# A selective scan beside a mixture of experts: TensorE spreads delta first in each slot, and du three units ahead of the scan

## The chip, the cores and the metric

The kernel runs on one NeuronCore of a Trainium2 chip. Its time is the device time of one execution in microseconds (us), as a median over runs. All times of the trace come from one profiled execution. The engines are named as the profile names them: PE is TensorE, DVE is VectorE, ACT is ScalarE, POOL is GpSimd, SP is the queue that issues most DMAs.

## What is computed

The input holds 32 sequences of 256 tokens of 128 numbers. After a layer norm, two blocks are added to it: a Mamba-like block with a selective scan, and a mixture of 8 experts. The scan is what matters here:

```python
def step(s, inp):
    d_t, u_t, B_t, C_t = inp
    dA = jnp.exp(d_t[..., None] * A)
    s = s * dA + (d_t * u_t)[..., None] * B_t[:, :, None, :]
    y_t = jnp.einsum('bhdn,bhn->bhd', s, C_t)
    return (s, y_t)
...
y = y + x * Dskip
y = y * jax.nn.silu(z)
out = y @ out_proj_w.T
```

There are 256 inner channels d and 16 states n for each, so 4096 recurrences run over the tokens. `delta` (`d_t` above) is a softplus of a projection of x; du stands for `d_t * u_t`. The experts are two matrix products with a relu between them, on 1024 gathered rows each.

## The kernel before

**Chunks, units, slots.** The tokens are cut into 16 chunks (`CHUNKS`) of 512. In a chunk the 4096 recurrences are 32 units (`SLOTS`) of 128 partitions: 8 channels times 16 states. Unit w of a chunk takes four steps, each one instruction on a tile of 128x512:

- PE spreads du, 8 channels to 128 partitions, with a 0/1 matrix `sel_d` (`spread_du`, L1243), into one of two PSUM banks (`du_ps[w % 2]`). It spreads delta in the same way (`spread_delta`, L1250), into one of three banks (`decay_of(w)`).
- ACT makes the decay, exp(delta * A), in place in that bank (L863).
- DVE multiplies the spread du by B (`spread_u`, L1020), which makes `u_sb`, and runs the scan over decay and `u_sb` (L1075).
- POOL multiplies the result by C (L647), and four units at a time are summed by PE (`sum_quad`, L1265).

**Order within an engine.** Every engine has a written-out order, a loop over chunks and 32 slots a chunk, and waits on semaphores. In its slot w, DVE first does `spread_u` of unit w+1, then the scan of unit w, then what else is due (the gates, L1000 and L1004, in slots 4 and 5 of each half of a chunk, and the addition of the output projection, L1011). ACT makes the decay of unit w in its slot w and then all other activations that are due. PE in its slot w first spreads for unit w+2 (`AHEAD = 2`), du and then delta, then sums a quad where one is due, and then does the parts of other tiles that the tables of the planner put into this slot.

**What the spreads wait for.** A du spread for unit v needs its bank read by DVE: it waits until `u_sb` of unit v-2 is made (`u_ready`). A delta spread for unit v needs its bank read by the scan of unit v-3 (`scan_done`). Since the three decay banks start anew in each chunk, the delta spread of a chunk's unit 0 waits for unit 30 of the chunk before, that of unit 1 for unit 31, and that of unit 2 finds its bank long free.

```python
wait(pe, "u_ready", per_chunk(ch, SLOTS, w - 1))
...
last = w - 2 if w >= 3 else (-1, 0, -2)[w]
wait(pe, "scan_done", per_chunk(ch, SLOTS, last))
```

**The other tiles.** In parallel with the scan of a chunk, PE makes the tiles of the next chunk, in two PSUM banks (`misc`): z0 and x0 (L1161, L1158; x takes four matmuls, `in_proj`), from them bc0 and v0 (L1169, `x_proj`), the softplus part D0 (L1178, L1180, `delta`), and the same for half 1 (z1, x1, bc1, v1, D1). Their slots are in `STAGE_A`: z0 in slot 4 and read by ACT in its slot 6, v0 in slot 9, z1 in 13, x1 in slots 11 to 14 and read in slot 16, v1 in 23. ACT's silu of z and x (`silus`, L726, L728, L730) loads its function table and puts the old one back, 1.28 us each. After v come the steps of the softplus (`softplus_step`, L748 to L762). In chunks 2 to 14 the experts' tiles (L1207 to L1218 on PE, L779 to L801 on ACT) are in slots of their own (`FFN_AT`); this table repeats after three chunks. `outp` (L1192) is the output projection, in slots 18 and 19. The first halves' D tiles of chunks 0 to 2 are taken further by DVE (`scale_x`, L1027), later ones by POOL (L587).

In what follows "unit 7" is unit 7 of its chunk, and slots are PE's slots if not said otherwise.

Of the kernel before, what the change touches and what calls it, by code (L numbers as in the profile page):

```python
# [34 lines left out]
CHUNKS = TOK // CH  # L35
# [5 lines left out]
SLOTS = HALVES * UNITS  # L41
# [5 lines left out]

HELP = {0: 1, 1: 1, CHUNKS - 1: 1}
SUM = QUADS + 2
AHEAD = 2  # L50
EXP, FF = 8, 512
CAP = TOK // EXP
FT = FF // P
# [72 lines left out]
def bass_mamba_moe(nc, hidden, in_w, conv_w, conv_b, xp_w, dt_w, dt_b, a_log, d_skip, out_w,  # L126
                   wg, w1, b1, w2, b2, consts, out):
    ctx = ExitStack()
    with ctx:
# [209 lines left out]
        def per_chunk(ch, n, k):  # L339
            return ch * n + k  # L340
# [12 lines left out]
        def wait(eng, name, value):  # L353
            if not isinstance(value, int) or value > 0:
                eng.wait_ge(S[name] if isinstance(name, str) else name, value)
# [11 lines left out]
        def head_of(w):  # L367

            return w % QUADS // 2

        def group_of(w):

            return w % 2 * QUADS + w % UNITS // QUADS
# [36 lines left out]
        def decay_of(w):  # L410
            return decay[w % len(decay)]
# [692 lines left out]
        def _(pe):  # L1104
# [117 lines left out]
            def tile_part(x, part):  # L1222

                if part == 0:
                    claim(x)
                if x.kind in ("x", "z"):
                    in_proj(x, part)
                elif x.kind == "D":
                    delta(x, part)
                elif x.kind in ("bc", "v"):  # L1230
                    x_proj(x)
                elif x.kind == "outp":
                    out_proj(x, part)
                else:
                    expert(x, part)

            def spread_du(ch, w):

                hf = w // UNITS
                if w % UNITS == 0:  # L1240
                    pe.wait_ge(S["stacked"], per_chunk(ch, 128, 64 * (hf + 1)))
                wait(pe, "u_ready", per_chunk(ch, SLOTS, w - 1))
                pe.matmul(du_ps[w % 2][:, :], sel_d[:, group_of(w), :, :].rearrange("k n d -> k (n d)"),  # L1243
                          dsp[:, hf, head_of(w), 1, :], start=True, stop=True).then_inc(S["du_spread"], 1)

            def spread_delta(ch, w):

                last = w - 2 if w >= 3 else (-1, 0, -2)[w]
                wait(pe, "scan_done", per_chunk(ch, SLOTS, last))
                pe.matmul(decay_of(w)[:, :], sel_d[:, group_of(w), :, :].rearrange("k n d -> k (n d)"),  # L1250
                          dsp[:, w // UNITS, head_of(w), 0, :], start=True, stop=True
                          ).then_inc(S["delta_spread"], 1)

            def spread(ch, w):
                spread_du(ch, w)
                spread_delta(ch, w)

            def sum_quad(ch, k):

                r = k % (UNITS // QUADS)  # L1260
                if r == 0:
                    wait(pe, "g_ready", per_chunk(ch, 2, k * QUADS // UNITS))
                wait_products(pe, ch, QUADS * (k + 1))
                for q in range(QUADS):
                    mm = pe.matmul(y_ps[q * 32:(q + 1) * 32, :], con[:, K_SUM + 32 * r:K_SUM + 32 * (r + 1)],  # L1265
                                   s_sb[:, (QUADS * k + q) % S_RING, :],
                                   start=(r == 0), stop=(r == UNITS // QUADS - 1))
                mm.then_inc(S["sum_done"], 1)
# [78 lines left out]
            first_tile("bc", 1)  # L1347
            first_tile("v", 1)
            pe.wait_ge(S["route_dve"], 5)
            for w in range(AHEAD):  # L1350
                spread(0, w)

            for ch in range(CHUNKS):
                for w in range(SLOTS):
                    if w + AHEAD < SLOTS:
                        spread(ch, w + AHEAD)
                    elif ch + 1 < CHUNKS:
                        spread(ch + 1, w + AHEAD - SLOTS)
                    if (w - SUM) % QUADS == 0:
                        if w >= SUM:  # L1360
                            sum_quad(ch, (w - SUM) // QUADS)
                        elif ch > 0:
                            sum_quad(ch - 1, (w - SUM) // QUADS + SLOTS // QUADS)
                    for x, part in parts_at.get(ch * SLOTS + w, []):
                        tile_part(x, part)
# [49 lines left out]
```

## Time and profile before

| | |
|---|---|
| median of 3 runs | 1085.64 us (1085.16 to 1087.5) |
| the profiled execution | 1085.05 us |
| its span, first to last instruction | 1083.2 us |
| mean granted TensorE clock | 0.956 |
| busy: DVE | 1014.2 us, 94% of the span |
| busy: PE matmuls / weight loads | 962.7 us, 89% / 440.5 us, 41% |
| busy: POOL | 898.0 us, 83% |
| busy: ACT | 747.5 us, 69% |
| one scan (L1075), one product for u_sb (L1020), 512 each | 1213 ns, 671 ns in the mean |
| the mean DMA rate | 99 GB/s |

The busy shares are averages over the whole program. The main loop over the units runs from 59.5 us, when DVE first makes `u_sb`, to 1068 us, when it has begun the last scan. Matmuls are pipelined, so the share of PE is not that of its peak; a matmul's start and end in the trace overlap those of its neighbours. An instruction's idle time is that of its engine just before it, with the engine or transfer whose signal ended it.

### The profile page before, as it was taken

What the parts mean: (1) busy time and instruction counts of PE and PEld (TensorE: products, weight loads), DVE (VectorE), ACT (ScalarE), POOL (GpSimd) and SP (SyncE); (2) the same over time, 40 slices, a digit from 0 to 9 for tenths busy, and PEclk for the clock granted to TensorE, in tenths of its full rate; (3) what the DMA queues carried; (4) which work ended last, traced back from release to release, by engine and by line L of the source; (5) the groups of instructions that cost most, each with busy time, mean ns of one, the idle gap of its engine ahead of it and who ended that gap; (6) DMA issues with size and microseconds to landing.
All of it is one profiled execution on the core that took longest, in us unless ns stands there. A gap on an engine that the chain in (4) does not pass through costs nothing.

```text
span 1083.2 us, 11968 instructions
## 1 busy us (share of the span) xinstructions
PE 962.7 (89%) x3521; PEld 440.5 (41%) x3521; DVE 1014.2 (94%) x1371; ACT 747.5 (69%) x1198; POOL 898.0 (83%) x783
## 2 busy tenths in 40 slices
PE   6978778799899999989999999999999999998785
PEld 3433223344444444434344444434444444443232
DVE  7789999999999999999999999999999999999995
ACT  5666465577887777786776877786787778786331
POOL 5458888997989898888888988888898888889874
PEclk8988998989999999999999999999999999999866
DMA  9584244344335342432533352243354233237821
GB/s 271 163 214 93 71 102 105 74 113 94 82 78 126 79 88 49 115 66 68 122 83 83 68 123 63 56 114 83 78 119 94 46 83 75 57 79 165 193 64 49
DMA packets 77452, 106.99 MB, mean 99 GB/s; under 512 B 8734, under 2 KB 46540, under 8 KB 77388
## 3 DMA queue, kind: packets, MB, share of 16 engines
q1 hardware_dynamic: 72944, 97.74, 40.5%
q0 software_dynamic: 4096, 8.46, 2.3%
q8 instruction: 29, 0.48, 0.2%
q14 instruction: 35, 0.29, 0.1%
q10 hardware_dynamic: 348, 0.03, 0.0%
HBM read 17.99 MB, written 21.10 MB: 36 GB/s over the span
## 4 chain that ended last, share of the span: by engine, by line
PE 35%; DVE 26%; issue 17%; ACT 15%; POOL 7%; DMA 0%; POOLq 0%; DVEq 0%; ACTq 0%
DVE u_sb L1020 11%; DVE s_sb L1075 8%; PE bank L1213 5%; PE bank L1250 4%; PE bank L1158 4%; PE bank L1265 4%; POOL s_sb L647 4%; PE bank L1243 4%; PE bank L1178 4%; ACT bank L863 3%; PE bank L1210 3%; PE bank L1169 2%; ACT L730 2%; ACT L726 2%; POOL moe L620 1%
## 5 line engine op out<-in xcount | busy, mean ns | idle before, releaser
L647 POOL TENSOR_TENSOR s_sb<-s_sb,c_of 128x512 f32<-128x512 f32 x488 | 625.0, 1290 | 122.2 <-DVE s_sb L1075 116.5
L1075 DVE TENSOR_TENSOR_SCAN s_sb<-bank,u_sb 128x512 f32<-128x512 f32 x512 | 620.9, 1213 | 14.2 <-ACT bank L863 14.0
L863 ACT ACTIVATE bank<-bank,a_neg 128x510 f32<-128x510 f32 x512 | 332.3, 663 | 213.4 <-PE bank L1250 211.7
L1020 DVE TENSOR_TENSOR u_sb<-bank,b_of 128x512 f32<-128x512 f32 x512 | 343.5, 671 | 24.9 <-PE bank L1243 23.8
L1243 PE MATMUL bank<-dsp,sel_d 128*128 128x512 f32 x512 | 326.3, 637 | 18.1 <-DVE u_sb L1020 16.7
L1250 PE MATMUL bank<-dsp,sel_d 128*128 128x512 f32 x512 | 228.2, 446 | 55.0 <-DVE s_sb L1075 51.9
L1243 PEld LDWEIGHTS bank<-dsp,sel_d 128*128 128x128 f32 x512 | 100.1, 195 | 194.3 <-DVE u_sb L1020 103.0
L1250 PEld LDWEIGHTS bank<-dsp,sel_d 128*128 128x128 f32 x512 | 100.2, 196 | 182.0 <-DVE s_sb L1075 136.6
L1265 PE MATMUL bank<-s_sb,con 128*32 128x512 f32 x1024 | 144.9, 639 | 17.4 <-POOL s_sb L647 13.4
L1158 PE MATMUL bank<-xnT,wx 128*128 128x512 f32 x256 | 133.8, 608 | 0.0
L653 POOL DMA_INDIRECT expert_in<-xn,put_at x64 | 70.1, 1096 | 11.6 <-issue 11.3
L620 POOL DMA_INDIRECT moe<-xn x64 | 64.7, 1010 | 12.9 <-issue 9.2
L1210 PE MATMUL bank<-xn 128*128 128x512 f32 x128 | 66.4, 611 | 4.7 <-ACT xn L779 4.7
L597 POOL TENSOR_TENSOR dd<-dd,hi 128x1024 fp32r<-128x1024 f32 x27 | 64.0, 2369 | 7.1 <-ACT hi L775 7.1
L1213 PE MATMUL bank<-xn 128*128 128x512 f32 x128 | 63.3, 602 | 0.0
L1158 PEld LDWEIGHTS bank<-xnT,wx 128*128 128x128 f32 x256 | 47.8, 192 | 27.1 <-issue 19.4
L785 ACT ACTIVATE xn<-bank,b1c 128x512 f32<-128x512 f32 x64 | 43.6, 700 | 18.8 <-PE bank L1210 18.8
L726 ACT ACT_TABLE_LOAD x32 | 41.1, 1283 | 15.4 <-PE bank L1161 15.0
L1265 PEld LDWEIGHTS bank<-s_sb,con 128*32 128x32 f32 x1024 | 20.9, 110 | 59.4 <-issue 39.1
L1192 PEld LDWEIGHTS bank<-wzo,g_sb 128*128 128x128 f32 x256 | 35.1, 204 | 18.0 <-issue 15.9
L730 ACT ACT_TABLE_LOAD x32 | 41.1, 1283 | 0.6
L1178 PE MATMUL bank<-sp_e,con 128*128 128x512 f32 x64 | 34.8, 626 | 6.7 <-ACT xn L785 6.0
(143 smaller groups left out, 1014.2 us busy)
## 6 DMA issues: line engine op xcount, KB each, us to landing
b_of<-bc SPq DMA_DIRECT2D x64, 256.0 KB, 5.5
c_of<-bc SPq DMA_DIRECT2D x64, 256.0 KB, 5.9
dsp<-hi SPq DMA_DIRECT2D x64, 256.0 KB, 4.1
dsp<-dd SPq DMA_DIRECT2D x64, 256.0 KB, 4.7
expert_in<-fill SPq DMA_DIRECT2D x16, 260.0 KB, 5.4
xn<-expert_in SPq DMA_DIRECT2D x8, 520.0 KB, 5.3
moe<-fill SPq DMA_DIRECT2D x8, 512.0 KB, 6.8
xn<-L_ffn_W SPq DMA_DIRECT2D x16, 256.0 KB, 5.0
```

Source lines behind the costliest of these rows:

```text
L620: pool.indirect_dma_start(moe[:, :], bass.IndirectOffsetOnAxis(ap=xe[:, e % 2, th * CT + q, DM + 1:ROWX].bitcast(U32), axis=0), eo[:, th, ...
L647: pool.tensor_tensor(s_now, s_now, c_of[:, hf, hh, :], ALU.mult).then_inc(S["p_ready"], 1)
L863: act.activation(d, d, ACT.Exp, scale=a_neg[:, k:k + 1]).then_inc(S["decay_ready"], 1)
L1020: dve.tensor_tensor(u_sb[:, w % U_RING, :], du_ps[w % 2][:, :], b_of[:, hf, head_of(w), :], ALU.mult).then_inc(S["u_ready"], 1)
L1075: dve.tensor_tensor_scan(s_sb[:, w % S_RING, :], decay_of(w)[:, :], u_sb[:, w % U_RING, :], 0.0, ALU.mult, ALU.add).then_inc(S["scan_done" ...
L1158: mm = pe.matmul(t[:, :], wx[:, hf, part, :], xnT[:, seqs, part:part + SEQ], start=(part == 0), stop=(part == TAPS - 1))
L1178: pe.matmul(t[:, :], ident, (sp_e, sp_r, sp_a)[part], start=(part == 0), stop=False)
L1210: mm = pe.matmul(t[:, :], w1_sb[:, b, x.k * P:(x.k + 1) * P], xeT, start=True, stop=True)
L1213: mm = pe.matmul(t[:, :], w2_sb[:, b, part, :], hT[:, part, :], start=(part == 0), stop=(part == FT - 1))
L1243: pe.matmul(du_ps[w % 2][:, :], sel_d[:, group_of(w), :, :].rearrange("k n d -> k (n d)"), dsp[:, hf, head_of(w), 1, :], start=True, stop= ...
L1250: pe.matmul(decay_of(w)[:, :], sel_d[:, group_of(w), :, :].rearrange("k n d -> k (n d)"), dsp[:, w // UNITS, head_of(w), 0, :], start=True ...
L1265: mm = pe.matmul(y_ps[q * 32:(q + 1) * 32, :], con[:, K_SUM + 32 * r:K_SUM + 32 * (r + 1)], s_sb[:, (QUADS * k + q) % S_RING, :], start=(r ...
```

## The change

The function `spread` that put du before delta is gone, and so is `AHEAD`. In its slot w, PE now spreads delta for unit w+2 first, as far ahead as before, and then du for unit w+3. Ahead of the loop du is spread for one more unit. The banks and what each spread waits for stay as they are: a du spread still waits for `u_sb` of the unit two before it, which for unit w+3 is unit w+1.

```diff
-AHEAD = 2
+
+DELTA_AHEAD, DU_AHEAD = 2, 3
...
-            def spread(ch, w):
-                spread_du(ch, w)
-                spread_delta(ch, w)
...
-            for w in range(AHEAD):
-                spread(0, w)
+            for w in range(DELTA_AHEAD):
+                spread_du(0, w)
+                spread_delta(0, w)
+            for w in range(DELTA_AHEAD, DU_AHEAD):
+                spread_du(0, w)
...
                 for w in range(SLOTS):
-                    if w + AHEAD < SLOTS:
-                        spread(ch, w + AHEAD)
-                    elif ch + 1 < CHUNKS:
-                        spread(ch + 1, w + AHEAD - SLOTS)
+                    for spread, ahead in ((spread_delta, DELTA_AHEAD), (spread_du, DU_AHEAD)):
+                        if w + ahead < SLOTS:
+                            spread(ch, w + ahead)
+                        elif ch + 1 < CHUNKS:
+                            spread(ch + 1, w + ahead - SLOTS)
                     if (w - SUM) % QUADS == 0:
```

The matmuls are the same; only their order on PE differs. Behind the spreads, PE's lines are numbered differently after the change (the du spread is L1244, the delta spread L1251, the sum of a quad L1262, and L1169 is L1170, L1213 is L1214, L1178 is L1179).

The first place is PE in slots 6 to 8 of chunk 5, around the scan of unit 7. Banks 3 and 4 hold du, 0 to 2 the decays, 5 the sums, 6 and 7 the other tiles. Before:

```order
L1243 MATMUL bank3<-dsp,sel_d 128x512 [waits u_ready]
L1250 MATMUL bank2<-dsp,sel_d 128x512 [waits scan_done]
L1265 MATMUL bank5<-s_sb,con 32x512 [waits p_ready,p_dve,g_ready]
L1265 MATMUL bank5<-s_sb,con 32x512 x3
L1243 MATMUL bank4<-dsp,sel_d 128x512 [waits u_ready]
L1250 MATMUL bank0<-dsp,sel_d 128x512 [waits scan_done]
L1169 MATMUL bank7<-xs,bcw 64x512 [waits misc_act]
L1213 MATMUL bank6<-xn 128x512 [waits misc_act]
L1243 MATMUL bank3<-dsp,sel_d 128x512 [waits u_ready]
L1250 MATMUL bank1<-dsp,sel_d 128x512 [waits scan_done]
L1213 MATMUL bank6<-xn 128x512 [waits misc_act] x2
```

And after the change:

```order
L1251 MATMUL bank2<-dsp,sel_d 128x512 [waits scan_done]
L1244 MATMUL bank4<-dsp,sel_d 128x512 [waits u_ready]
L1262 MATMUL bank5<-s_sb,con 32x512 [waits p_ready,p_dve,g_ready]
L1262 MATMUL bank5<-s_sb,con 32x512 x3
L1251 MATMUL bank0<-dsp,sel_d 128x512 [waits scan_done]
L1244 MATMUL bank3<-dsp,sel_d 128x512 [waits u_ready]
L1170 MATMUL bank7<-xs,bcw 64x512 [waits misc_act]
L1214 MATMUL bank6<-xn 128x512 [waits misc_act]
L1251 MATMUL bank1<-dsp,sel_d 128x512 [waits scan_done]
L1244 MATMUL bank4<-dsp,sel_d 128x512 [waits u_ready]
L1214 MATMUL bank6<-xn 128x512 [waits misc_act] x2
```

The spread that stands last ahead of a slot's other work, and so holds it back while it waits, was the delta spread with its wait for a scan; it is now the du spread with its wait for a product `u_sb`.

The second place is PE at the boundary between chunks 4 and 5 (slots 30 and 31 of chunk 4). Before:

```order
L1243 MATMUL bank3<-dsp,sel_d 128x512 [waits u_ready,stacked]
L1250 MATMUL bank0<-dsp,sel_d 128x512 [waits scan_done]
L1265 MATMUL bank5<-s_sb,con 32x512 [waits p_ready,p_dve]
L1265 MATMUL bank5<-s_sb,con 32x512 x3
L1210 MATMUL bank7<-xn 128x512 [waits misc_act]
L1243 MATMUL bank4<-dsp,sel_d 128x512 [waits u_ready]
L1250 MATMUL bank1<-dsp,sel_d 128x512 [waits scan_done]
```

And after the change:

```order
L1251 MATMUL bank0<-dsp,sel_d 128x512 [waits scan_done]
L1244 MATMUL bank4<-dsp,sel_d 128x512 [waits u_ready]
L1262 MATMUL bank5<-s_sb,con 32x512 [waits p_ready,p_dve]
L1262 MATMUL bank5<-s_sb,con 32x512 x3
L1211 MATMUL bank7<-xn 128x512 [waits misc_act]
L1251 MATMUL bank1<-dsp,sel_d 128x512 [waits scan_done]
L1244 MATMUL bank3<-dsp,sel_d 128x512 [waits u_ready]
```

The du spread of unit 1 (bank 4) has moved from behind the sum and an expert's matmul to ahead of them.

## Rows read from the trace of the kernel before

**Rows 1.** Stretches of the run: busy time of each engine, granted clock, DMA share, GB/s.
```profile
132.00:192.00 60.00, 49.16 (x164) 19.85 (x163) 59.57 (x72) 37.10 (x56) 52.76 (x45) 0.91 0.44 96
312.00:372.00 60.00, 56.53 (x215) 26.28 (x215) 57.86 (x70) 45.54 (x72) 51.36 (x43) 1.00 0.42 93
```

**Rows 2.** Who waited for whom, whole span: total us, times, longest.
```profile
DVE u_sb L1020 <- PE bank L1243: 23.8, 45, 1.9
DVE s_sb L1075 <- ACT bank L863: 14.0, 28, 1.0
```

**Rows 3.** Timeline, chunk boundary: start, us, engine, line, [idle before <-releaser].
```profile
387.00 0.49 PE L1250 MATMUL bank<-dsp,sel_d 128*128 128x512 f32 x1 [0.25 <-DVE s_sb L1075]
...
389.81 0.69 DVE L1020 TENSOR_TENSOR u_sb<-bank,b_of 128x512 f32<-128x512 f32 x1 [1.13 <-PE bank L1243]
```

**Rows 4.** Timeline, from tile z0 to the scan of unit 7 of chunk 5.
```profile
399.81 0.39 PE L1250 MATMUL bank<-dsp,sel_d 128*128 128x512 f32 x1
...
399.83 1.28 ACT L726 ACT_TABLE_LOAD   x1 [1.10 <-PE bank L1161]
...
400.04 0.40 PE L1243 MATMUL bank<-dsp,sel_d 128*128 128x512 f32 x1
...
403.61 1.23 ACT L863 ACTIVATE bank<-bank,a_neg 128x510 f32<-128x510 f32 x2
...
404.30 1.22 DVE L1075 TENSOR_TENSOR_SCAN s_sb<-bank,u_sb 128x512 f32<-128x512 f32 x1 [0.56 <-ACT bank L863]
```

**Rows 5.** Timeline, TensorE meets the scan, before and after unit 7.
```profile
401.95 1.21 DVE L1075 TENSOR_TENSOR_SCAN s_sb<-bank,u_sb 128x512 f32<-128x512 f32 x1
...
403.08 0.67 DVE L1020 TENSOR_TENSOR u_sb<-bank,b_of 128x512 f32<-128x512 f32 x1
...
403.22 0.50 PE L1250 MATMUL bank<-dsp,sel_d 128*128 128x512 f32 x1 [0.24 <-DVE s_sb L1075]
...
403.65 1.07 PE L1169 MATMUL bank<-xs,bcw 128*64 128x512 f32 x2
...
405.44 0.67 DVE L1020 TENSOR_TENSOR u_sb<-bank,b_of 128x512 f32<-128x512 f32 x1
...
406.08 1.88 PE L1213 MATMUL bank<-xn 128*128 128x512 f32 x4
...
410.18 0.69 ACT L748 ACTIVATE sp_a<-bank,b1c 128x512 f32<-128x512 f32 x1 [0.17 <-PE bank L1169]
```

**Rows 6.** Timeline, the scan of unit 17.
```profile
422.60 1.81 ACT L863 ACTIVATE bank<-bank,a_neg 128x510 f32<-128x510 f32 x3
423.29 1.22 DVE L1075 TENSOR_TENSOR_SCAN s_sb<-bank,u_sb 128x512 f32<-128x512 f32 x1 [0.95 <-ACT bank L863]
```

**Rows 7.** Who waited for whom, VectorE, 378 to 563 us.
```profile
DVE u_sb L1020 <- PE bank L1243: 5.2, 10, 1.1
DVE s_sb L1075 <- ACT bank L863: 3.4, 7, 1.0
```

**Rows 8.** Timeline, chunk 5, unit 28, and the boundary after it.
```profile
443.02 0.68 ACT L863 ACTIVATE bank<-bank,a_neg 128x510 f32<-128x510 f32 x1
...
443.99 1.21 DVE L1075 TENSOR_TENSOR_SCAN s_sb<-bank,u_sb 128x512 f32<-128x512 f32 x1
...
449.32 0.69 DVE L1020 TENSOR_TENSOR u_sb<-bank,b_of 128x512 f32<-128x512 f32 x1 [0.44 <-PE bank L1243]
```

**Rows 9.** Timeline, chunk 2: softplus part and unit 17; chunk 7: unit 28.
```profile
204.05 1.81 DVE L1027 TENSOR_TENSOR dd<-dd,xs 128x512 f32<-128x512 f32 x1 [0.55 <-ACT dd L769]
...
238.77 1.22 DVE L1075 TENSOR_TENSOR_SCAN s_sb<-bank,u_sb 128x512 f32<-128x512 f32 x1 [0.47 <-ACT bank L863]
...
565.43 0.71 ACT L863 ACTIVATE bank<-bank,a_neg 128x510 f32<-128x510 f32 x1
...
566.23 1.22 DVE L1075 TENSOR_TENSOR_SCAN s_sb<-bank,u_sb 128x512 f32<-128x512 f32 x1
...
567.96 0.69 DVE L1020 TENSOR_TENSOR u_sb<-bank,b_of 128x512 f32<-128x512 f32 x1 [0.51 <-PE bank L1243]
```

## The prediction

> **What bounds the kernel.** I read the stretches first, then the waits, then the timeline around every stall of VectorE (DVE). In a middle stretch of 60 us DVE is busy for 57.86 us and TensorE (PE) for 56.53 us; in an early one DVE is busy for 59.57 us [rows 1]. So DVE sets the pace, and what can be won in the middle is the little that it stands: 23.8 us in 45 waits for a du spread, 14.0 us in 28 waits for a decay from ScalarE (ACT) [rows 2]. The change aims at the first kind.
>
> The timeline shows where they arise. At a chunk boundary PE meets the scan (its delta spread starts at 387.00 us, just when the scan that it waits for has ended), then does a sum and an expert's matmul, and only then the next du spread; DVE gets it 1.13 us late [rows 3]. From there PE does not stand again until it has made tile z0. ACT stands 1.10 us for that tile, loads its tables and does two silus, and makes the decay of unit 7 only at 403.61 us; DVE waits another 0.56 us for it [rows 4]. That is the reading on which all else rests: **the second stall hangs from PE's work and ACT's, not from DVE's progress.** If the first stall goes, DVE arrives earlier at unit 7 and waits there longer, by the same 1.13 us. The same again ten units later: PE meets a scan, makes v0, ACT stands 0.17 us for it [rows 5] and is then busy without a gap to the decays at 422.60 us, where DVE waits 0.95 us, a du stall having come shortly before [rows 6].
>
> **What the change does to a meeting.** Where PE lags behind by more than about 0.6 us, the order matters little: both spreads are free to go. Where it has caught up, it now waits twice. Delta starts 0.06 us after the scan that it waits for (that ends at 401.95 + 1.21 = 403.16 us, delta starts at 403.22). The du spread behind it waits for the product that DVE makes right after that scan: it starts at 403.08 and ends at 403.75 us [rows 5]. With the same 0.06 us, du starts at 403.81, **0.59 us after delta**, and all other work of the slot stands behind it on PE; no other engine's queue is held, but ACT waits for these tiles. So a meeting costs up to 0.59 us on the path PE, ACT, decay, scan. At the meeting after unit 7 it is less, since PE comes a little late: the product ends at 405.44 + 0.67 = 406.11 us, du starts at 406.17, and, 0.43 us later (403.22 to 403.65 was the same step), the experts' matmul at 406.60 in place of 406.08 [rows 5]: 0.52 us.
>
> Two smaller prices. At a chunk boundary the delta spread of unit 0 waits for the youngest scan, while du of unit 1 needs a product that is long made; there the extra spread costs only its own time, 0.23 us (the distance of two spreads, 399.81 to 400.04) [rows 4]. And where the decay hangs directly from a delta spread, delta being first in its slot gives back that 0.23 us: 0.59 - 0.23 = 0.36 us. From below, a meeting costs nothing where the tile is not awaited; it could gain only the 0.23 us. From above it is 0.59 us, plus the gate operation where one stands ahead of the product on DVE. I take each place at what its own rows give.
>
> **The sum over one period.** The experts' plan repeats after three chunks; I follow 378 to 563 us, where DVE waits 5.2 us for du and 3.4 us for decays [rows 7]. For each stall I ask what comes late next:
> - boundary to unit 7 (stalls 1.13 + 0.56 us): they merge into one at unit 7, as z0 comes 0.23 us later: +0.23 us;
> - unit 7 to unit 17 (one du stall, and decay stalls up to the 0.95 us): they merge at unit 17, v0 comes 0.52 us later than the scan does: +0.52;
> - unit 17 to the boundary: here ACT's decay for unit 28 is made at 443.02 + 0.68 = 443.70 us and its scan starts at 443.99, so 0.29 us of the 0.59 us is hidden: +0.30. The du stall after it, 0.44 us at 449.32 [rows 8], goes for good: together -0.14;
> - boundary to unit 7 of chunk 6: +0.23;
> - unit 7 to 17 of chunk 6: three du stalls and one decay stall merge; PE is held there by a product of GpSimd (POOL) in place of a scan, so there is no meeting: 0;
> - to unit 7 of chunk 7: meeting with delta's 0.23 us back: +0.36;
> - to unit 17 of chunk 7, the same kind of meeting: +0.36;
> - to the end of chunk 7: the decay for unit 28 ends at 565.43 + 0.71 = 566.14 us, its scan starts at 566.23 [rows 9]: 0.09 us hidden, +0.50; the du stall of 0.51 us at 567.96 goes: together -0.01.
>
> Sum +1.55 us a period. The pattern runs from 238 to 977 us, four periods: +6.2 us. In chunks 0 to 2, DVE's own part of the softplus waits for ACT (0.55 us at 204.05), hanging from PE's work behind a boundary: three times 0.23, +0.7. The silus before unit 17 end just in time or late (0.47 us at 238.77) [rows 9]: three times 0.36, +1.1. In chunk 15 the longest du stall, 1.9 us [rows 2], goes, but the addition of the output projection, which DVE does two instructions later, waits for the matmuls that stood before that du spread; I take 0.
>
> Total 6.2 + 0.7 + 1.1 + 0 = +8.0 us on the profiled execution's 1085.05 us, so **1093.0 us**. That execution is 0.6 us under the median shown, well inside what the forecast can tell.
>
> **A rule weighed.** Rows 1 have PE busy for 56.53 of 60 us, and for 26.28 us with weight loads. The Trainium skill (page "Perfetto Trace Analysis", section "Identifying the Most-Contended Engine") says that matmul busy time is a poor measure and that TensorE's headroom is better judged by weight-load time. By it PE would have more than half its time free, DVE alone would bind, and its waits would be the thing to remove: the first rival, not my forecast. What speaks against it here is ACT standing for z0 and v0.
>
> **The rivals.**
> - *The du stalls go for good* (faster). Deciding point: whether, after a du stall is gone, the next decay is made early enough to keep DVE from standing there. If units 7 and 17 get their tiles early enough, 23.8 us less the 1.9 us of chunk 15: 1063 us; if half comes back, 1074 us. For it: in several units after a stall the decay has more than a microsecond in hand. Against it: the merged stalls above. 0.12.
> - *Handed back, nothing more.* The du stalls turn into decay stalls, and the second wait of a meeting is hidden, because PE soon lags again: 1085 us, within 2 us. 0.09.
> - *The clock falls.* The granted clock is 1.00 in the dense stretch and 0.91 where PE stands more [rows 1]. If PE's added waits took it to 0.91, its 56.5 us of 60 would become 62, 2 us over each 60, some 12 times: about 1085 + 25 = 1110 us. PE's waits grow by under 1% of the span, so 0.03.
> - *My forecast*, meetings on the path: 0.76. That the change doesn't do what it says has a part in it: the third unit of lead exists only where PE lags; after a meeting du is as early as DVE's product allows.
>
> **Numbers.** Low end: the second rival, 1085. High end: six meetings a period at the full 0.59 us and two boundaries at 0.23 us, +4.0 us, four times, with the start 1103; I take 1099, since two places show what they hide. Left out: the first rival (0.12), clock and extremes (0.06). A measurement of this kernel tells about 0.2% (2.2 us) from no change. Faster 0.12, same 0.09, slower 0.79.
>
> **What would show it.** DVE's waits for du (line 1020) fall from 23.8 to under 3 us. Its waits for decays (line 1075) rise from 14.0 to about 14 + 21 + 8 = 43 us, most at units 7 and 17. PE has new waits for `u_sb` at its du spread, about 0.3 us each in slots where it has caught up, in chunks 0, 1 and 15 too. DVE's busy time stays at 1014 us and the clock at 0.95. The forecast is wrong if the decay waits stay below 30 us, or if the meeting after unit 7 of chunk 5 doesn't show du about 0.6 us behind delta.

## The result, and the profile after

The changed kernel takes 1095.55 us (median of 5 runs, 1093.77 to 1099.08) against 1085.64 us (the same median with five runs of before). The ratio over the runs of both is 1.0088, with a 95% interval of 1.0065 to 1.0111. The forecast was slower, 1093.0 us, between 1085 and 1099. The profiled execution of after took 1098.07 us (span 1096.2 us, mean granted clock 0.953), 2.5 us more than its median. So the trace shows a loss of 13.0 us where the runs show 9.9; both are used below, and not mixed.

The page's busy times, after:

```profile
PE 969.6 (88%) x3521; PEld 442.3 (40%) x3521; DVE 1011.2 (92%) x1371; ACT 745.3 (68%) x1198; POOL 897.7 (82%) x783
```

Stretches of after (us, busy PE, PEld, DVE, ACT, POOL, granted clock, DMA share, GB/s), for [rows 1]:

```profile
132.00:192.00 60.00, 45.78 (x161) 19.70 (x163) 58.61 (x71) 35.72 (x54) 52.85 (x44) 0.97 0.44 97
312.00:372.00 60.00, 56.60 (x212) 25.69 (x213) 56.83 (x68) 45.01 (x72) 50.66 (x42) 1.00 0.42 92
```

DVE's busy time is 1.03 us lower in the second stretch and PE's the same: nothing works longer, DVE stands longer. The waits of the whole span of after (us in total, times, longest), for [rows 2]:

```profile
PE bank L1244 <- DVE u_sb L1021: 52.1, 58, 3.4
DVE s_sb L1076 <- ACT bank L864: 43.6, 39, 1.9
PE bank L1251 <- DVE s_sb L1076: 30.0, 60, 1.2
DVE acc L1012 <- PE bank L1196: 8.2, 2, 5.6
...
DVE s_sb L1076 <- issue: 4.0, 8, 0.5
...
DVE u_sb L1021 <- PE bank L1244: 0.5, 2, 0.3
```

The waits for du went from 23.8 to 0.5 us, and those for decays from 14.0 to 43.6 us. So 23.3 us were taken away and 29.6 us came back on the other wait; 38.3 us of it, in 33 waits, stand between 250 and 980 us. The 4.0 us that the profile puts down to nothing ("issue") are decay waits too: all eight are at unit 28, and each of these scans starts 0.09 us after ACT has made its decay. The addition of the output projection (L1012) waits 2.8 us longer than before. PE's waits for products are not all new either, since before had these:

```profile
PE bank L1243 <- DVE u_sb L1020: 16.7, 14, 3.4
```

The long decay waits stand at two kinds of place. This is the first in after, from z0 to unit 7 of chunk 5 and the meeting behind it (for [rows 4, 5]):

```profile
404.64 1.28 ACT L727 ACT_TABLE_LOAD   x1 [1.34 <-PE bank L1162]
...
405.60 0.50 PE L1244 MATMUL bank<-dsp,sel_d 128*128 128x512 f32 x1 [0.34 <-DVE u_sb L1021]
...
408.42 1.81 ACT L864 ACTIVATE bank<-bank,a_neg 128x510 f32<-128x510 f32 x3
...
409.11 1.22 DVE L1076 TENSOR_TENSOR_SCAN s_sb<-bank,u_sb 128x512 f32<-128x512 f32 x1 [1.85 <-ACT bank L864]
...
410.39 0.50 PE L1251 MATMUL bank<-dsp,sel_d 128*128 128x512 f32 x1 [0.52 <-DVE s_sb L1076]
...
410.97 0.50 PE L1244 MATMUL bank<-dsp,sel_d 128*128 128x512 f32 x1
411.31 1.88 PE L1214 MATMUL bank<-xn 128*128 128x512 f32 x4
...
415.41 0.69 ACT L749 ACTIVATE sp_a<-bank,b1c 128x512 f32<-128x512 f32 x1 [0.17 <-PE bank L1170]
```

ACT stands 1.34 us for z0 (1.10 before) and makes the decay of unit 7 3.78 us after the table load begins, exactly as long as before. The stalls of 1.13 and 0.56 us have merged into one of 1.85 us. At the meeting du comes 0.58 us behind delta. ACT gets v0 6.30 us after unit 7's scan began, before 5.88 us (410.18 - 404.30): 0.42 us later. The second place, for [rows 6]:

```profile
427.83 1.81 ACT L864 ACTIVATE bank<-bank,a_neg 128x510 f32<-128x510 f32 x3
428.52 1.22 DVE L1076 TENSOR_TENSOR_SCAN s_sb<-bank,u_sb 128x512 f32<-128x512 f32 x1 [1.51 <-ACT bank L864]
```

1.51 us in place of 0.45 and 0.95 us.

### The profile page after: what moved, and what is told of

Same layout as the page of the kernel before. It is cut to its first block, busy times and chain, and to the rows that moved or that the text cites. A ratio compares the mean times of both kernels' runs of the same rounds, so it can differ in the third digit from the quotient of the medians.

```text
span 1096.2 us, 11968 instructions
## 1 busy us (share of the span) xinstructions
PE 969.6 (88%) x3521; PEld 442.3 (40%) x3521; DVE 1011.2 (92%) x1371; ACT 745.3 (68%) x1198; POOL 897.7 (82%) x783
## 4 chain that ended last, share of the span: by engine, by line
PE 38%; ACT 23%; DVE 19%; issue 16%; POOL 3%; DMA 0%; POOLq 0%; DVEq 0%; ACTq 0%
DVE u_sb L1021 10%; ACT bank L864 6%; PE bank L1159 5%; PE bank L1244 5%; PE bank L1262 4%; PE bank L1251 4%; PE bank L1214 4%; PE bank L1179 3%; PE bank L1170 3%; PE bank L1211 3%; ACT L731 3%; ACT L727 3%; DVE s_sb L1076 2%; POOL s_sb L648 2%; PE bank L1162 2%
## 5 line engine op out<-in xcount | busy, mean ns | idle before, releaser
L1076 DVE TENSOR_TENSOR_SCAN s_sb<-bank,u_sb 128x512 f32<-128x512 f32 x512 | 619.7, 1211 | 49.4 <-ACT bank L864 43.6
L1251 PE MATMUL bank<-dsp,sel_d 128*128 128x512 f32 x512 | 320.9, 627 | 30.3 <-DVE s_sb L1076 30.0
L1244 PE MATMUL bank<-dsp,sel_d 128*128 128x512 f32 x512 | 226.8, 443 | 59.3 <-DVE u_sb L1021 52.1
L1251 PEld LDWEIGHTS bank<-dsp,sel_d 128*128 128x128 f32 x512 | 100.6, 196 | 231.8 <-DVE s_sb L1076 142.0
L1244 PEld LDWEIGHTS bank<-dsp,sel_d 128*128 128x128 f32 x512 | 101.0, 197 | 166.5 <-DVE u_sb L1021 109.6
L1262 PE MATMUL bank<-s_sb,con 128*32 128x512 f32 x1024 | 144.8, 639 | 9.0 <-POOL s_sb L648 9.0
L786 ACT ACTIVATE xn<-bank,b1c 128x512 f32<-128x512 f32 x64 | 43.6, 700 | 30.3 <-PE bank L1211 30.3
L1214 PE MATMUL bank<-xn 128*128 128x512 f32 x128 | 63.4, 602 | 0.0
L1193 PEld LDWEIGHTS bank<-wzo,g_sb 128*128 128x128 f32 x256 | 35.2, 205 | 18.1 <-issue 16.7
L588 POOL TENSOR_TENSOR dd<-dd,xs 128x512 f32<-128x512 f32 x27 | 34.5, 1278 | 9.7 <-ACT dd L770 9.4
L1262 PEld LDWEIGHTS bank<-s_sb,con 128*32 128x32 f32 x1024 | 20.7, 109 | 50.6 <-issue 50.6
```

The source lines that it names most:

```text
L1076: dve.tensor_tensor_scan(s_sb[:, w % S_RING, :], decay_of(w)[:, :], u_sb[:, w % U_RING, :], 0.0, ALU.mult, ALU.add).then_inc(S["scan_done" ...
L1214: mm = pe.matmul(t[:, :], w2_sb[:, b, part, :], hT[:, part, :], start=(part == 0), stop=(part == FT - 1))
```

## How late the scan is, unit by unit

A loss that builds up slowly is best read from the start of the same scan in two traces. Each number is the start of one unit's scan in the timeline less its start before (before: 79.58, 209.93, 238.77, 404.30, 588.87, 958.00, 1020.22, 1049.22 us). The runs' names are explained below. "Net" is the last column less the first.

| | ch.0 unit 7 | ch.2 unit 3 | ch.2 unit 17 | ch.5 unit 7 | ch.8 unit 7 | ch.14 unit 7 | ch.15 unit 7 | ch.15 unit 21 | net |
|---|---|---|---|---|---|---|---|---|---|
| after | 0.34 | 0.33 | 2.56 | 4.81 | 6.47 | 10.69 | 12.04 | 12.72 | +12.4 |
| e1 | -0.06 | 0.16 | 2.06 | 3.86 | 5.82 | 9.65 | 9.85 | 10.30 | +10.4 |
| e11 | -0.06 | -0.02 | 1.73 | 2.30 | 2.23 | 2.12 | 2.88 | 1.14 | +1.2 |
| e2 | -0.13 | 0.18 | 0.86 | 0.92 | 0.79 | 0.59 | 1.22 | -0.15 | 0.0 |
| e4 | 0.45 | 0.49 | 0.98 | 0.89 | 0.83 | 0.63 | 0.99 | -0.41 | -0.9 |
| e6 | -0.61 | 1.32 | 0.44 | 3.56 | 6.93 | 13.80 | 16.27 | 14.66 | +15.3 |
| e9 | 1.56 | 1.63 | 0.36 | 0.00 | -0.04 | -0.09 | 0.49 | 0.53 | -1.0 |
| e7 | -0.89 | -0.84 | -0.66 | -1.99 | -2.69 | -4.01 | -3.22 | -5.18 | -4.3 |
| e5 | 1.48 | 2.27 | 2.22 | 1.23 | 0.16 | -1.98 | -1.83 | -2.47 | -4.0 |
| e10 | -0.32 | -0.08 | 0.65 | -1.67 | -3.42 | -6.95 | -5.64 | -5.88 | -5.6 |
| e8 | -0.84 | -0.78 | -0.83 | -3.02 | -4.61 | -7.80 | -6.98 | -7.77 | -6.9 |

The first column differs by up to 2.5 us between kernels. Up to 1.5 us of that is the single execution and not the kernel (e5 has the order of before up to there, and is yet 1.48 us later), so the net says more than the span.

Between unit 7 of chunk 5 and of chunk 8 after loses 1.66 us. But three things weren't forecast. The first is chunk 2, where it loses 2.2 us up to unit 17. These are the rows of after there:

```profile
211.39 3.06 DVE L1039 TENSOR_TENSOR dd<-dd,hi 128x1024 fp32r<-128x1024 f32 x1
...
214.37 0.68 DVE L1021 TENSOR_TENSOR u_sb<-bank,b_of 128x512 f32<-128x512 f32 x1
...
215.11 0.50 PE L1244 MATMUL bank<-dsp,sel_d 128*128 128x512 f32 x1 [3.08 <-DVE u_sb L1021]
...
216.49 1.91 PE L1162 MATMUL bank<-xnT,wzo 128*128 128x512 f32 x2
...
218.49 1.28 ACT L727 ACT_TABLE_LOAD   x1 [5.76 <-PE bank L1162]
...
222.96 1.22 DVE L1076 TENSOR_TENSOR_SCAN s_sb<-bank,u_sb 128x512 f32<-128x512 f32 x1 [1.52 <-ACT bank L864]
```

and the same place before:

```profile
211.06 3.05 DVE L1038 TENSOR_TENSOR dd<-dd,hi 128x1024 fp32r<-128x1024 f32 x1
...
211.53 1.02 PE L1158 MATMUL bank<-xnT,wx 128*128 128x512 f32 x2
...
212.39 1.02 PE L1161 MATMUL bank<-xnT,wzo 128*128 128x512 f32 x2
...
213.49 1.28 ACT L726 ACT_TABLE_LOAD   x1 [1.10 <-PE bank L1161]
```

DVE's part of the softplus, 3.05 us in one instruction, stands between the scan and the next product. Before, PE made x0 and z0 meanwhile. After, PE waits 3.08 us for the product with x0 and z0 behind it, and ACT starts on z0 5.0 us later (218.49 in place of 213.49). The decay of unit 7 had over 3 us in hand, so 1.52 us are left to see. Not all of the 5.0 us is the wait. x0's last part starts 3.92 us later than before (215.45 in place of 211.53); the other 1.1 us is the clock: z0's two matmuls take 1.91 us in place of 1.02, at a granted clock of 0.64 between 215 and 219 us (before, 1.00 between 211 and 215 us). In e1 and e11, which also wait 3.1 us there, z0 falls into a stretch at the low level as well.

The second is chunks 3 and 12. Units 7 to 17 cost 0.75 us in chunk 3 and 0.69 us in chunk 12, while in chunks 6 and 9, which have the same place in the plan, the scan wins back 0.2 us. Here are the first matmuls of the experts' tile behind the meeting after unit 7, in chunk 3 and in chunk 6, and the stretches around them (the granted clock is the third number from the end):

```profile
287.62 1.75 PE L1211 MATMUL bank<-xn 128*128 128x512 f32 x2
...
474.82 1.02 PE L1211 MATMUL bank<-xn 128*128 128x512 f32 x2
```

```profile
288.00:291.00 3.00, 3.00 (x5) 1.14 (x4) 3.00 (x5) 0.69 (x1) 2.81 (x3) 0.50 0.06 22
...
475.00:478.00 3.00, 2.33 (x10) 0.96 (x13) 3.00 (x5) 2.04 (x5) 2.80 (x4) 1.00 0.06 22
```

In chunk 3 PE runs at the low level (0.50, 1.2 GHz) there, the same matmuls take 1.75 us in place of 1.02, and ACT gets v0 7.40 us after unit 7's scan in place of 5.83. DVE then waits 0.63 us at unit 12 and 0.51 us for a decay at unit 14, and in chunk 6 it has neither (only one of 0.27 us, for du). Chunk 12 has the same (0.50 between 848 and 851 us, and 0.49 and 0.51 us at units 12 and 14), chunk 9 has not (1.00 between 662 and 665 us). Between 250 and 980 us these are the only two stretches at the low level in the trace of after, and before has none. Against chunks 6 and 9 they cost 0.95 and 0.90 us. Why the clock fell in these two and not in the other two isn't shown: in all four, PE's matmuls from 20 us ahead of unit 7's scan up to that meeting start at the same times, within 0.12 us.

The third is chunk 15, where the delay grows by 1.6 us, from 11.11 us at the end of chunk 14 to 12.72 us. Behind unit 20 it grows by 0.68 us: the longest du stall is gone as forecast, but DVE waits at the addition:

```profile
1060.74 0.69 DVE L1012 TENSOR_TENSOR acc<-bank,acc 128x512 f32<-128x512 f32 x1 [2.56 <-PE bank L1196]
```

Another 0.84 us is no wait at all. Between the scans of units 1 and 2 DVE itself multiplies a scan's result by C (L1083), and that takes 1.51 us in place of 0.67, beside a POOL instruction that began at 1018.67 us:

```profile
1018.97 1.51 DVE L1083 TENSOR_TENSOR s_sb<-s_sb,c_of 128x512 f32<-128x512 f32 x1
```

Before, DVE's product began at 1007.80 us, when that POOL instruction (1006.54 us, 1.27 us long) was all but over. The later it begins beside it, the shorter it is: 0.30 us after POOL's start 1.51 us, 0.61 us after it 1.21 us (e9), 1.03 us after it 0.79 us (e4), and 1.26 us after it 0.67 us (before).

## The experiments

The kernels measured here compute the same as the kernel before. There is no time for e3: it was e6 without the wait for a half chunk's data, and leaves that wait out.

**e1: the second wait alone.** The order of before; PE only waits, behind the spreads of each slot, for the product that the changed du spread would wait for.

```diff
                         spread(ch + 1, w + AHEAD - SLOTS)
+                    if w + 3 < SLOTS or ch + 1 < CHUNKS:
+                        wait(pe, "u_ready", per_chunk(ch, SLOTS, w + 2))
```

> The order of before, with one thing added: after its delta spread PE waits in each slot until DVE has made the product of unit w+1, which is what the moved du spread waits for. No spread is moved, du is two units ahead. Theory (the second wait of a meeting is the price): slower than before by 6 to 14 us, 1092 to 1100 us, since the meeting costs its 0.59 us and the du stalls stay too: DVE's waits for du stay above 20 us and its decay waits grow. Rival (the price is in the moved matmul itself or in the clock): within 2 us of before.

Measured: 1095.8 us (1093.91 to 1097.89), ratio 1.0091 [1.0068, 1.0114], as expected. Waits of e1:

```profile
DVE u_sb L1020 <- PE bank L1243: 27.7, 55, 2.3
DVE s_sb L1075 <- ACT bank L863: 16.6, 32, 1.1
```

No du spread is earlier than before, so nothing is gained at it, and the whole loss is there. So PE's wait alone is enough for the loss, and in the changed kernel the du stalls that went bought nothing net. The delay doesn't arise in the same places, though: in e1 the stalls at units 7 and 17 are as before (0.58 and 0.97 us in chunk 5). That the two totals agree so closely is in part chance.

**e2: the boundary alone.** The du of a chunk's unit 1 goes one slot earlier, behind the spreads of unit 0.

```diff
-                        spread(ch + 1, w + AHEAD - SLOTS)
+                        if w + AHEAD == SLOTS:
+                            spread(ch + 1, 0)
+                            spread_du(ch + 1, 1)
+                        else:
+                            spread_delta(ch + 1, 1)
```

> The order of before, but at each chunk boundary the du spread of the next chunk's unit 1 is put one slot earlier, ahead of the sum and the expert's matmul; there it waits for nothing. Theory (stalls merge at unit 7): the du stalls of 1.13 and 0.62 us at unit 1 vanish, the decay stall at unit 7 grows by as much and by 0.23 us, DVE's waits stay the same in sum or grow a little; 1085 to 1089 us. Rival (du stalls go for good): 1.75 us less in each of four periods, about 1078 us.

Measured: 1086.79 us (1084.15 to 1088.85), ratio 1.0007 [0.9997, 1.0016]. The stall of 1.13 us at unit 1 of chunk 5 [rows 3] is now one unit further on, and unit 7 waits 0.71 us in place of 0.56:

```profile
392.26 0.69 DVE L1020 TENSOR_TENSOR u_sb<-bank,b_of 128x512 f32<-128x512 f32 x1 [0.98 <-PE bank L1243]
...
405.22 1.22 DVE L1075 TENSOR_TENSOR_SCAN s_sb<-bank,u_sb 128x512 f32<-128x512 f32 x1 [0.71 <-ACT bank L863]
```

The time is as expected, but the stall didn't vanish: 0.98 us of it moved, and the other 0.15 us came back at unit 7.

**e4: du a unit further ahead, but behind the first piece of the slot's work.** Delta opens the slot; du of w+3 is inserted behind the sum or the first part of a tile.

```diff
-                    for spread, ahead in ((spread_delta, DELTA_AHEAD), (spread_du, DU_AHEAD)):
+                    now(spread_delta, DELTA_AHEAD)
...
+                    work += [(tile_part, x, part) for x, part in parts_at.get(ch * SLOTS + w, [])]
+                    work.insert(1, (now, spread_du, DU_AHEAD))
+                    for do, *what in work:
+                        do(*what)
```

> As the change, but in each slot the du spread of unit w+3 stands behind the first piece of other work (the sum of a quad, or the first matmuls of a tile) in place of ahead of it; that piece takes 0.4 to 1.0 us, in which the product is made. Theory: the second wait of a meeting is gone, the 0.23 us of the extra spread stays where a slot has two pieces: 1083 to 1089 us, PE's waits for the product at the du spread under 15 us in place of 52, DVE's waits for du under 8 us. Rival (the cost is in the longer lead or in the swap, not in the wait): above 1091 us.

Measured: 1085.33 us (1083.77 to 1086.56), ratio 0.9986 [0.9975, 0.9998]. Waits of e4:

```profile
DVE s_sb L1076 <- ACT bank L864: 26.3, 30, 1.5
PE bank L1244 <- DVE u_sb L1021: 15.9, 17, 3.4
DVE u_sb L1021 <- PE bank L1244: 12.6, 31, 1.2
```

PE's waits for products fall from 52.1 to 15.9 us, about what they were before (16.7 us), and the 10 us are back. With the second wait hidden, the third unit of lead is worth next to nothing (the second rival): DVE waits 11.2 us less for du than before and 12.3 us more for decays. The time was as expected; the du waits of 12.6 us were not, I had expected under 8.

**e6: delta first, both two units ahead.** The third unit of lead is taken away, the swap kept; delta gets the wait for a half chunk's data that du had made ahead of it.

```diff
-DELTA_AHEAD, DU_AHEAD = 2, 3
+DELTA_AHEAD, DU_AHEAD = 2, 2
...
+                if w % UNITS == 0:
+                    pe.wait_ge(S["stacked"], per_chunk(ch, 128, 64 * (w // UNITS + 1)))
```

> Delta ahead of du in each slot, both two units ahead (with the wait for the stacked operands at the first delta of a half too). Theory: du comes 0.23 us later and delta 0.23 us earlier, so DVE's waits for du rise from 23.8 to 28 to 34 us, its decay waits fall below 12 us, and the time is 1084 to 1089 us. Rival (the swap itself is what costs 9 us): 1092 us and more.

Measured: 1102.81 us (1099.45 to 1103.58), ratio 1.0151 [1.0131, 1.0170]: missed by far, and so were the du waits (45.2 us for 28 to 34). Waits of e6, and its meeting before unit 7 of chunk 5:

```profile
PE bank L1253 <- DVE s_sb L1076: 102.3, 141, 3.0
DVE u_sb L1021 <- PE bank L1244: 45.2, 68, 1.6
DVE s_sb L1076 <- ACT bank L864: 6.7, 12, 0.7
```

```profile
406.85 0.50 PE L1253 MATMUL bank<-dsp,sel_d 128*128 128x512 f32 x1 [0.58 <-DVE s_sb L1076]
407.19 0.40 PE L1244 MATMUL bank<-dsp,sel_d 128*128 128x512 f32 x1
407.51 1.07 PE L1170 MATMUL bank<-xs,bcw 128*64 128x512 f32 x2
```

I had taken the swap for free, or nearly. Before, the du of the same unit was spread 0.73 us ahead of delta, in the time that PE would otherwise stand for the scan, and only delta (403.22) and the work (403.65 [rows 5]) came behind the meeting:

```profile
402.49 0.49 PE L1243 MATMUL bank<-dsp,sel_d 128*128 128x512 f32 x1
```

Swapped, both spreads come behind it: the work starts 0.66 us after delta in place of 0.43, and the du spread itself is late for DVE. PE waits 102.3 us for scans in place of 51.9. So du first is not a habit but a filler of idle time, and the third unit of lead in the change does repair something: a damage that the swap does.

**e5: the lead only where a stall goes for good.** The order of before, with du of w+3 at the end of the spreads in nine slots: chunk 15 slot 18; slot 27 of chunks 4, 7, 10, 13; slot 29 of chunks 2, 5, 8, 11.

```diff
...
+                        if t - 1 not in early:
+                            spread_du(*divmod(t + AHEAD, SLOTS))
+                        spread_delta(*divmod(t + AHEAD, SLOTS))
+                        if t in early:
+                            spread_du(*divmod(t + AHEAD + 1, SLOTS))
```

> The order of before, but du is put a unit further ahead in nine slots alone: in chunk 15 ahead of the output projection (unit 21), in chunks 4, 7, 10 and 13 into slot 27, where PE stands over a microsecond for ACT anyway (unit 30), and in chunks 2, 5, 8 and 11 into slot 29 (unit 0 of the next chunk). Theory: chunk 15 gives 1.4 us as in the run with du second, the others at most 0.25 us each since PE is held by ACT at the next boundary: 1 to 3.5 us faster than before, 1083 to 1085.5 us. Rival (every du stall comes back later): no faster than before by more than 0.5 us.

Measured: 1081.69 us (1080.73 to 1082.7), ratio 0.9952 [0.9937, 0.9968]. That is better than expected. The table has it: 1.07 us a period between chunks 5 and 14, and 0.64 us in chunk 15; this trace began 1.5 us late. The net in the trace is 4.0 us, the ratio gives 5.2 us, and I had expected 1 to 3.5. What goes at unit 30 or 0 here is not handed back at unit 7, whose stall stays at 0.56 to 0.58 us in eight chunks and falls from 0.25 to about 0.15 us in chunks 3, 6, 9 and 12: what stands behind the boundary, PE's way to z0 too, runs as much earlier as the scan.

**e7, e8, e9, e10: z0 earlier.** If unit 7 hangs from z0, making z0 earlier must take its stall away. In slot 4 PE makes the last part of x0 and then z0; now z0 comes first. The order of x1 and z1 stays, since x1's last part stands a slot behind z1.

```diff
...
+        for parts in parts_at.values():
+            if [x.kind for x, part in parts] == ["x", "z"] and parts[0][1] == TAPS - 1:
+                parts.reverse()
```

e7 is this on the kernel before, e8 on e4, e9 on the changed kernel, e10 on e5.

> The spreads as before; in slot 4 of each chunk PE makes tile z0 ahead of the last matmul of x0 in place of behind it, so ACT gets z0 0.86 us earlier and x0 0.86 us later, while it loads its table and does z0's silu (1.9 us). Theory (unit 7 hangs from z0): the decay stalls at unit 7 (0.24 to 0.57 us in each of chunks 3 to 14) vanish, 4 to 6 us faster than before, 1080 to 1083 us; DVE's decay waits fall from 14.0 to about 9 us. Rival (unit 7 is held by something else, such as ACT's own work): no change.

> z0 ahead of x0's last matmul as in the run with z first, and the du spread three units ahead behind the first piece of other work. Theory: with unit 7 untied from PE by 0.86 us, the du stalls at the boundary are no longer all handed back there: the unit-7 stalls of 1.2 and 0.4 us in the run with du second fall to about 0.35 and 0, that is 6 to 10 us less than that run, 1075 to 1080 us. Rival (an early du gains nothing anywhere): no faster than z first alone.

> The changed kernel, with tile z0 (and z1) made ahead of the last matmul of x0 (x1) where both stand in one slot. My theory: in the changed kernel, too, the scan of unit 7 hangs from z0 through two table loads and two silus, so its decay stalls (up to 1.8 us, chunks 1 to 14) shrink by what z0 comes earlier, 0.4 to 0.86 us each, and nothing later hands it back in full. Expected 0.5 to 0.9% under the changed kernel: 1085 to 1090 us. Rival (the second spread's waits of the changed order are the limit everywhere, and z0 is not what unit 7 waits for): no gain, 1094 to 1097 us.

> The kernel before, with z0 ahead of x0's last matmul, and du a unit further ahead only in the slots where the longest stalls for it were seen to go for good (chunk 15 slot 18; slot 27 of chunks 4, 7, 10, 13; slot 29 of chunks 2, 5, 8, 11). If the two gains are independent, they add: 0.35% and 0.2 to 0.48% below the kernel before, 1077 to 1081 us. If z first already shifts TensorE against the scan so that the chosen slots are no longer those with the stalls, it is no better than z first alone: 1082 us.

| | us | ratio to before |
|---|---|---|
| e7 | 1082.45 | 0.9965 [0.9954, 0.9976] |
| e8 | 1078.96 | 0.9929 [0.9910, 0.9949] |
| e9 | 1085.77 | 0.9996 [0.9986, 1.0006] |
| e10 | 1079.83 | 0.9938 [0.9923, 0.9953] |

All four times lie in the ranges expected. In e7 and e10 the stall at unit 7 is gone from every chunk.

Timeline of e9, z0 to unit 7 of chunk 5:

```profile
399.82 1.28 ACT L730 ACT_TABLE_LOAD   x1 [0.48 <-PE bank L1165]
...
403.61 1.81 ACT L867 ACTIVATE bank<-bank,a_neg 128x510 f32<-128x510 f32 x3
404.30 1.22 DVE L1079 TENSOR_TENSOR_SCAN s_sb<-bank,u_sb 128x512 f32<-128x512 f32 x1 [0.99 <-ACT bank L867]
```

Waits of e9, then of e8:

```profile
PE bank L1247 <- DVE u_sb L1024: 50.1, 59, 3.4
DVE s_sb L1079 <- ACT bank L867: 29.8, 31, 1.7
```

```profile
PE bank L1247 <- DVE u_sb L1024: 18.6, 18, 3.4
DVE s_sb L1079 <- ACT bank L867: 16.2, 17, 1.5
```

ACT stands 0.48 us for z0 in e9, not 1.34, and unit 7 waits 0.99 us, not 1.85: the same 0.86 us. PE's waits for products are as long as in the changed kernel (50.1 and 52.1 us), yet the time is 9.8 us shorter and back at that of before. So most of what PE's second wait costs, it costs because z0 stands behind it. Not all: e7 has z0 early too, without the second wait, and e9 is 3.3 us slower (1085.77 against 1082.45; the nets of the two traces, -1.0 and -4.3, say the same). About a third of the loss stays with z0 out of the way. e8 beats both kernels and is the best version found, with e10 within its interval.

**e11: the wait of e1 in chunks 2 and 15 alone.**

```diff
+                    if ch in (2, CHUNKS - 1) and (w + 3 < SLOTS or ch + 1 < CHUNKS):
+                        wait(pe, "u_ready", per_chunk(ch, SLOTS, w + 2))
```

> The order of before, with TensorE's wait for the product of unit w+1 behind the spreads in chunks 2 and 15 alone, which are two places that my forecast priced at 0.4 and 0 us. If what the trace of the changed kernel shows there (delays of 1.5 and 0.7 us grown beside the stall that went) is the price of the second wait, the scans of chunk 3 to 14 are late by 1 to 2.5 us and the end by 2 to 4 us: 1088 to 1090 us. If the price there is as I forecast, it is 0.4 us and can't be told from the kernel before: 1085 to 1087 us.

Measured: 1085.75 us (1084.87 to 1089.96, 12 runs), ratio 1.0003 [0.9992, 1.0014]; missed in the time, held in half of the trace. Chunk 2 costs 2.3 us (its wait of 3.07 us stands ahead of x0's last part and z0, which then runs at the low level), and that stays, flat, to chunk 14. At unit 0 of chunk 15 0.8 us are added; e2, which has no such wait, stands 0.75 us there too. At unit 21 1.7 us are given back, and what gave them back is the clock. Stretches around the eight matmuls of the output projection there: before, after, and e11.

```profile
1041.00:1046.00 5.00, 5.00 (x25) 3.52 (x18) 3.13 (x4) 0.42 (x2) 5.00 (x5) 0.57 0.17 52
```

```profile
1053.00:1058.00 5.00, 4.97 (x20) 2.87 (x21) 5.00 (x6) 0.04 (x1) 5.00 (x5) 0.50 0.17 52
```

```profile
1042.00:1047.00 5.00, 3.82 (x26) 2.35 (x26) 4.92 (x7) 1.18 (x2) 4.18 (x4) 1.00 0.26 77
```

Those eight matmuls take 1.23 + 1.06 us at about 1.2 GHz (clock 0.57 before, 0.50 after) and 0.71 + 0.61 us at 2.4 GHz (e11). From the start of the sum ahead of them to the next du spread PE takes 4.45 us before and 2.36 us in e11, for the same work: the 2.09 us between them are more than the whole stall of before. With the low level DVE stood 1.87 us for du behind them (before), 2.27 us (e1), or 2.56 us for the sum of after; in e11 and e7 (1.00) not at all, in e2 (0.84) 0.49 us. So the stall of 1.87 us that I had weighed in chunk 15 came in the main from the clock of that one execution. Whether the price of chunk 2 is seen in the time of most executions is open: the trace has +2.3 us, and the medians, 1085.75 and 1086.59 (before, in the same runs), say nothing was lost.

## Why the prediction was right, and where it wasn't

- **"The second stall hangs from PE's work and ACT's, not from DVE's progress."** Held. e9 and e7 move z0, and unit 7's stall follows. In the changed kernel the du stalls go, and the stalls at units 7 and 17 grow by about as much. e2 shows it only in small: 0.15 us go at one place and come back at unit 7.
- **The meeting, 0.59 us.** Held: du is 0.58 us behind delta. What v0 loses by it was forecast as 0.52 and is 0.42 us. e1 shows this second wait alone to be worth the whole loss in the medians.
- **The sum over one period, +1.55.** +1.66 us from unit 7 of chunk 5 to that of chunk 8, by parts (forecast in brackets): 0.42 (0.52), then 0.13 to unit 7 of chunk 6 (-0.14 + 0.23 = 0.09), -0.20 (0), 0.62 (0.36), 0.41 (0.36), and 0.28 (-0.01 + 0.23 = 0.22). That the sum is closer than its terms is luck: the -0.20 and the 0.26 too much offset each other.
- **"The pattern runs from 238 to 977 us, four periods: +6.2."** Near for the mechanism, too small for the trace: from 2.56 us (unit 17 of chunk 2) the delay grows to 11.11 us (unit 17 of chunk 14), by 8.55 us. Of that, 1.85 us are the two stretches at the low clock in chunks 3 and 12. The other 6.7 us are four times the 1.66 us of the period measured.
- **"Three softplus parts 0.7, three silus 1.1."** The sum is near (1.8 against 2.2 from the first unit 7 on), the place is wrong. Chunk 1 costs nothing and chunk 2 2.2 us. The step that failed is "from above it is 0.59 us, plus the gate operation where one stands ahead of the product on DVE": in chunk 2 3.05 us of softplus stand there, which the wait of PE takes in whole. The low clock at z0 behind it adds another 1.1 us to z0's lateness; without it the stall of 1.52 us at unit 7 would be about 0.4 us (an estimate: 1.52 less 1.1).
- **"In chunk 15 ... I take 0."** The addition does take over the stall, as said (2.56 us for 1.87), so this term is 0.7 and not 0. With the slower product beside POOL the delay grows by 1.6 us in chunk 15 of the profiled execution. But the stall depends on the clock, and the median after is 2.5 us below the profiled execution.
- **The rule weighed** (the Trainium skill, page "Perfetto Trace Analysis", section "Identifying the Most-Contended Engine"). By it DVE's waits were the thing to remove. The numbers of after speak against it here: the weight loads of the dense stretch are 25.69 of 60 us, so PE looks half free, the du waits are gone, and the kernel is 0.9% slower. e4 and e9, which differ from the changed kernel only in the order of PE's work, take no longer than the kernel before.
- **What would show it.** du waits under 3 us: 0.5. Decay waits about 43: 43.6, or 47.6 with the eight at unit 28. New waits for `u_sb` "about 0.3 us each": there are 52.1 us in 58, against 16.7 us in 14 before, so 35.4 us in 44 are new, 0.8 us each. That is nearly three times the forecast. At the meeting after unit 7 they are 0.34 to 0.38 us in most chunks, but elsewhere PE waits out a whole product of 0.67 us, or what DVE does ahead of it as well (3.08 us in chunk 2). DVE busy 1014: 1011.2; clock 0.95: 0.953 for the span.
- **The rivals.** "The du stalls go for good" fell; of the 45 stalls only the few that e5 picks do. "Handed back, nothing more" is what e4 shows when the second wait is hidden. "The clock falls" fell as it was put, for the middle stretch shown has 1.00 and not 0.91. But a small part of it came about: the two stretches at 0.50 in chunks 3 and 12, which the forecast had at nothing.

So the mechanism was right, and the middle was sized nearly right. The trace has 13.0 us against my 8.0: 2.6 against 1.8 us up to unit 17 of chunk 2 (0.3 us of it ahead of the first unit 7), 8.55 against 6.2 us in the four periods, and 1.9 against 0 us behind them. Most of the difference is what the forecast left out: the low clock at the tiles of chunks 2, 3 and 12, the addition, and DVE's product beside POOL. The medians have 9.9 us, and which of the three parts is smaller in the executions that weren't profiled can't be told.

## What to carry to other kernels

In an engine that works in order, a wait put ahead of other work costs what stands behind it, not what it waits for: before moving a fill of a freed buffer forward, look at what another engine awaits from the same slot. A filler that does its work while its engine would stand anyway (du ahead of the scan's wait) is worth its place, even where it looks interchangeable. And a stall is worth removing only if the next one doesn't hang from something that stays where it is: here, moving z0 ahead of x0's last part (0.35%), and hiding the wait as well (together 0.71%), did more than removing 23 us of stalls.

## What was not expected of the hardware

The granted clock of a stretch at the end differs between executions (0.50 to 1.00 around the same eight matmuls), and the mean over the span (0.956 before, 0.953 after, 0.957 in e11) doesn't show it. It is worth about 1 us of matmuls (2.29 or 1.32 us) and up to 2.6 us of DVE's standing. In the middle of the changed kernel two stretches at 0.50 (288 to 291 and 848 to 851 us), in chunks that otherwise repeat chunks 6 and 9, cost 0.9 us each, and the stretch of 60 us that one looks at first (1.00) doesn't show them either.

A DVE product of two tiles in SBUF took 0.67 us when it began as a POOL instruction ended, and 1.51 us when it began 0.30 us into a POOL instruction of 1.27 us. Also, the first scans of one execution start up to 1.5 us before or after those of another whose order is the same up to there, as much as many effects looked for here: compare the delays of units, not spans.
